# A four-block image kernel: row sums ahead of normalisations, clearing in pieces and hats placed by GpSimd at the end of the third block

## What is computed

```python
def _gn(v, G=32, eps=1e-05):               # per image, groups of two channels
    g = v.reshape(B_, G, C_ // G, H_, W_)
    return ((g - mean(g)) / sqrt(var(g) + eps)).reshape(v.shape)

# third block: attention of all 1024 pixels of an image with each other
e1, e2, asm = (prelu(conv1x1(x, w, b)) for w, b in ...)    # 32, 32 and 64 channels
score = softmax(einsum('nci,ncj->nij', e1, e2), axis=2)
out = einsum('nij,ncj->nci', score, asm)

# fourth block: bilinear shift by theta_s per channel, then 64 -> 64 channels
s = z1*(1-dy)*(1-dx) + z2*(1-dy)*dx + z3*dy*(1-dx) + z4*dy*dx
return einsum('bchw,oc->bohw', s * w_dw, w_pw)

x = x + L0(_gn(x)); x = x + L1(_gn(x)); x = x + L2(_gn(x)); x = x + L3(_gn(x))
```

## Time and profile before

| | before |
|---|---|
| median of 3 runs | 831.44 us (829.63 to 832.01) |
| the profiled execution | 829.34 us, span in the profile 827.5 us |
| PE / DVE / ACT / POOL busy | 84% / 72% / 48% / 50% |

### The profile page before, as it was taken

The page is one execution under the profiler, slowest core; times in us unless marked ns, Lnnn a source line. Parts: engine busy times, 40 slices in busy tenths (PEclk is TensorE's granted clock), DMA queues, the critical chain, the costliest instruction groups (busy, mean ns, idle before and its releaser), DMA issues.

```text
span 827.5 us, 9121 instructions
## 1 busy us (share of the span) xinstructions
PE 693.6 (84%) x2566; PEld 349.4 (42%) x2566; DVE 597.5 (72%) x943; ACT 398.0 (48%) x653; POOL 410.8 (50%) x242
## 2 busy tenths in 40 slices
PE   0875887887459999897989999998999999966787
PEld 0332322222147777574433434343434333225783
DVE  5686899999642325685787868685868787798746
ACT  1768557756211002103547474646566565735571
POOL 3123677677242115101695949494968768542100
PEclk9987899999769999997999999999999999987899
DMA  7000000000000000203303020120303030000005
GB/s 294 0 0 0 1 0 0 0 0 0 0 0 1 0 0 15 63 0 77 76 1 77 1 58 21 31 47 2 76 0 77 0 76 0 1 0 1 1 1 204
DMA packets 7961, 24.90 MB, mean 30 GB/s; under 512 B 2032, under 2 KB 2032, under 8 KB 7792
## 3 DMA queue, kind: packets, MB, share of 16 engines
q1 hardware_dynamic: 7920, 24.45, 10.7%
HBM read 6.09 MB, written 4.19 MB: 12 GB/s over the span
## 4 chain that ended last, share of the span: by engine, by line
PE 49%; DVE 30%; issue 12%; ACT 4%; POOL 2%; DMA 1%; SPq 1%; DVEq 1%; ACTq 0%; POOLq 0%
PE PS L1356 12%; PE PS L1433 10%; PE PS L1400 7%; PE PS L1422 4%; DVE SM L621 3%; PE PS L1381 3%; DVE PS L458 2%; DVE RB L467 2%; PE PS L1391 2%; DVE X L492 1%; PE PS L1268 1%; PE PS L1567 1%; PE PS L1363 1%; PE PS L1595 1%; DVE PS L475 1%
## 5 line engine op out<-in xcount | busy, mean ns | idle before, releaser
L621 DVE TENSOR_REDUCE SM<-PS 128x1 f32<-128x512 f32 x256 | 172.8, 687 | 78.1 <-PE PS L1400 74.1
L988 ACT ACTIVATE RB<-PS 128x512 f32<-128x512 f32 x256 | 139.2, 598 | 108.6 <-PE PS L1422 104.2
L1185 POOL TENSOR_TENSOR RB<-RB 128x1024 f32<-128x1024 f32 x66 | 156.3, 2385 | 20.8 <-ACT RB L988 12.8
L1400 PE MATMUL PS<-R 96*128 96x512 f32 x256 | 123.3, 482 | 13.8 <-DVE SM L621 10.0
L1356 PE MATMUL PS<-R,WS 128*128 128x512 f32 x432 | 119.0, 422 | 4.1 <-ACT R L952 4.1
L1356 PEld LDWEIGHTS PS<-R,WS 128*128 128x128 f32 x432 | 83.1, 193 | 30.9 <-issue 9.3
L1422 PE MATMUL PS<-R 98*128 98x512 f32 x256 | 87.6, 419 | 8.6 <-ACT R L994 4.1
L1400 PEld LDWEIGHTS PS<-R 96*128 96x128 f32 x256 | 48.9, 192 | 95.2 <-issue 49.8
L1433 PE MATMUL PS<-RB 128*64 128x512 f32 x320 | 87.1, 628 | 0.0
L1296 PE MATMUL PS<-RA,W 128*128 (+1 forms) x128 | 67.8, 658 | 21.1 <-DVE RB L467 15.1
L1422 PEld LDWEIGHTS PS<-R 98*128 98x128 f32 x256 | 47.7, 193 | 36.0 <-ACT RB L988 17.8
(11 more groups left out here) (171 smaller groups left out, 1172.4 us busy)
## 6 DMA issues: line engine op xcount, KB each, us to landing
R<-WS SPq DMA_DIRECT2D x84, 128.0 KB, 2.3
X<-x SPq DMA_DIRECT2D x8, 512.0 KB, 10.0
out<-X SPq DMA_DIRECT2D x7, 512.0 KB, 2.6
R<-R SPq DMA_DIRECT2D x24, 128.0 KB, 2.3
W<-pack SPq DMA_DIRECT2D x1, 1273.0 KB, 8.1
RB<-pack SPq DMA_DIRECT2D x1, 576.0 KB, 12.8
out<-X SPq DMA_DIRECT2D x2, 256.0 KB, 2.4
```

What stands on the lines that cost most here:

```text
L621: v.tensor_reduce(MX[:, par, tile, h:h + 1], bank(2 + h), AX.X, ALU.max)\
L988: act(slot[:, h * HALF:(h + 1) * HALF], bank(4 + h), ACT.Exp).then_inc(s["p_ready"], 1)
L1185: i = g.tensor_tensor(out, out, PT[j % SLOTS][par], ALU.add)
L1400: mm(bank(2 + h), stack(b, par, 0)[0:96, tile * P:(tile + 1) * P], stack(b, par, 1)[0:96, h * HALF:(h + 1) * HALF]).then_inc(s["s_mm"], 1)
```

## The change

On DVE, the two hats of group 0 are made right after the first adds of pair 7, ahead of pair 6's residual; the coefficients of `GN3A` come ahead of pair 6's statistics; DVE normalises pairs 0, 1 and 6 only, with an `add` between, and ACT pairs 2 to 5 and 7; DVE's `place(g)` is for the x matrices of groups 0, 2 and 3; both hats of group 1 follow the last `add`. The transposes use banks 2 to 5 instead of 0 to 3, and the group for `GN3B` on PE stands at n=7, not n=5. GpSimd clears the matrices in eight pieces of 128x1024, five of them ahead of its row sums of pair 7, and places the hats `(0,0)`, `(1,0)`, `(1,1)`, and makes and places the y hats of groups 2 and 3 itself; ACT has no part in the hats any more. Core of the diff (semaphores `g3_dve`, `g3_act`, `am_pool` take the place of `g3_done`, `am_act`):

```diff
@@ vector @@
+            hat(0, 0)
+            hat(0, 1)
             for h in range(2):
                 scaled(q, h)
                 residual(q, h)
             add(2)
-            hat(0, 0)
+            coefs_shift(GN3A, 0, q)
             end_stats(q, 0)
             end_stats(q, 1)
-            coefs_shift(GN3A, 0, q)
             add(3)
-            for p in range(q):
-                if p == 3:
-                    add(4)
-                normed3(p)
+            normed3(0)
+            add(4)
+            normed3(1)
             for j in (5, 6, 7):
                 add(j)
-            hat(0, 1)
             hat(1, 0)
+            hat(1, 1)
...
             normed3(q - 1)
-            v.wait_ge(s["am_zero"], 1)
-            place(0, 0)
-            place(0, 1)
+            place(0)
...
-                if n == 0:
-                    hat(1, 1)
-                    v.wait_ge(s["am_zero"], 2)
-                    place(1, 0)
-                    place(1, 1)
                 if n in (2, 6):
                     hat(2 + n // 6, 1)
                 if n in (4, 8):
-                    place(1 + n // 4, 1)
+                    place(1 + n // 4)
@@ scalar @@
             attend(PAIRS - 1, 1, lead=False)
+            a.wait_ge(s["coef_ready"], GN3A + 1)
+            for p in range(2, PAIRS - 2):
+                normed3(p)
             for h in range(2):
                 product_out(PAIRS - 1, h)
...
-                if n == 6:
+                if n == 8:
                     a.wait_ge(s["coef_ready"], GN3B + 1)
...
-                if n in (3, 7):
-                    place(2 + n // 7)
@@ gpsimd @@
+            def clear(k):
+                g.memset(RB[:, k * L:(k + 1) * L], 0.0).then_inc(s["am_zero"], 1)
                 if p == PAIRS - 1:
                     power(GN3A, 0, PAIRS - 2)
+                    g.wait_ge(s["v_done"], 2 * PAIRS)
+                    g.wait_ge(s["pv_done"], 2 * CHUNKS * (PAIRS - 2))
+                    for k in (13, 14, 15):
+                        clear(k)
+                    g.wait_ge(s["sum_mm"], 2 * PAIRS - 2)
+                    for k in (8, 9):
+                        clear(k)
...
+            def hat(gr):
+                tv = mat("thy", C)[:, gr * CG:(gr + 1) * CG].unsqueeze(2).to_broadcast([P, CG, WW])
+                link(g.tensor_tensor(HATP, grid, tv, ALU.add))
+                link(g.tensor_scalar(HAT[2], HATP, 0.0, 1.0, ALU.min, ALU.mult))
+                link(g.tensor_scalar(HATP, HATP, 0.0, 1.0, ALU.max, ALU.mult))
+                link(g.tensor_tensor(HAT[2], HAT[2], HATP, ALU.subtract))
+            def place(gr, a):
+                for q in range(4):
+                    r = slice(32 * q, 32 * q + 32)
+                    i = g.tensor_scalar(AM[gr % 2][a][r, :, 32 * q:32 * q + 32], HAT[2 * min(gr, 1) + a][r],
+                                        1.0 if gr >= 2 else 0.0, 0.0, ALU.add, ALU.max)
+                    if q < 3:
+                        link(i)
+                i.then_inc(s["am_pool"], 1)
+            g.wait_ge(s["pv_done"], 2 * CHUNKS * PAIRS)
+            clear(12)
+            g.wait_ge(s["sum_mm"], 2 * PAIRS)
+            for k in (10, 11):
+                clear(k)
+            g.wait_ge(s["am_zero"], 8)
+            g.wait_ge(s["hat_done"], 4)
+            place(0, 0)
+            power(GN3B, PAIRS - 2, PAIRS)
+            g.wait_ge(s["pow_done"], GN3B + 1)
+            place(1, 0)
+            place(1, 1)
             for gr in (2, 3):
+                hat(gr)
+                g.wait_ge(s["s1_mm"], (gr - 1) * CG // 4)
+                place(gr, 0)
@@ tensor @@
-            t.wait_ge(s["acc_read"], 2 * PAIRS)
+            t.wait_ge(s["s_read"], 32 * PAIRS)
+            t.wait_ge(s["p_ready"], 32 * PAIRS)
...
-                if n == 5:
+                if n == 7:
                     t.wait_ge(s["x2_done"], 2 * PAIRS)
                     group(GN3B, PAIRS - 2, PAIRS)
```

More of the change, by code:

```diff
@@ L281, in transposed_out @@
             q, xb = divmod(n, 8)
[L282 removed]
+            src = bank(2 + n % 4).rearrange("p (x a c) -> p x a c", x=4, a=2)
             dst = D.rearrange("p c (q a x) -> p q x a c", q=2, a=2)[:, q, 4 * xb:4 * xb + 4]
@@ L731, in hat @@
             def hat(g, a):
+                if g == 2:
+                    v.wait_ge(s["am_pool"], 3)
                 w = HAT[2 * min(g, 1) + a]
@@ L736, in hat, with place @@
                 link(v.tensor_scalar(w, HATV, -1.0, 1.0, ALU.mult, ALU.add))
-                link(v.scalar_tensor_tensor(w, HATV, 1.0, w, ALU.add, ALU.min))
-            def place(g, a):
-                if g >= 2:
+                v.scalar_tensor_tensor(w, HATV, 1.0, w, ALU.add, ALU.min).then_inc(s["hat_done"], 1)
+                v.wait_ge(s["hat_done"], 2 * g + a + 1 if g < 2 else 3 + g)
+            def place(g):
+                if g == 0:
+                    v.wait_ge(s["am_zero"], 8)
+                else:
                     v.wait_ge(s["s2_mm"], (g - 1) * CG // 4)
@@ L800, in _ @@
                 transposed_out(v.tensor_copy, n).then_inc(s["tr_dve"], 1)
+            v.wait_ge(s["am_pool"], 1)
             for n in range(16):
@@ L1041, in _, with normed3 @@
             attend(PAIRS - 1, 1, lead=False)
+            def normed3(p):
+                act(G3[:, p, :], X[:, p, :], ACT.Identity, scale=SC[:, p:p + 1], bias=SH[:, p:p + 1])\
+                    .then_inc(s["g3_act"], 1)
+            a.wait_ge(s["coef_ready"], GN3A + 1)
+            for p in range(2, PAIRS - 2):
+                normed3(p)
             for h in range(2):
@@ L1052, in _ @@
             for n in list(range(8)) + list(range(8, 16, 2)):
-                if n == 6:
+                if n == 8:
                     a.wait_ge(s["coef_ready"], GN3B + 1)
-                    act(G3[:, PAIRS - 1, :], X[:, PAIRS - 1, :], ACT.Identity, scale=SC[:, PAIRS - 1:PAIRS],
-                        bias=SH[:, PAIRS - 1:PAIRS]).then_inc(s["g3_done"], 1)
+                    normed3(PAIRS - 1)
                 a.wait_ge(s["tr_mm"], n + 1)
                 transposed_out(copy, n).then_inc(s["tr_act"], 1)
-            def place(g):
-                a.wait_ge(s["dist_done"], g - 1)
-                link(act(HAT[2], HAT[2], ACT.Abs))
-                a.wait_ge(s["s2_mm"], (g - 1) * CG // 4)
-                for q in range(4):
-                    r = slice(32 * q, 32 * q + 32)
-                    i = act(AM[g % 2][0][r, :, 32 * q:32 * q + 32], HAT[2][r], ACT.Relu, bias=ONE[r], scale=-1.0)
-                i.then_inc(s["am_act"], 1)
             for n in range(16):
@@ L1222, in _ @@
                 sums(p)
-            for n in range(2):
-                if n == 0:
-                    g.wait_ge(s["sum_mm"], 2 * PAIRS)
-                else:
-                    g.wait_ge(s["x2_done"], 2 * PAIRS)
-                g.memset(RB[:, PAIRS * L + 2 * n * CG * P:PAIRS * L + 2 * (n + 1) * CG * P], 0.0)\
-                    .then_inc(s["am_zero"], 1)
-                g.wait_ge(s["am_zero"], n + 1)
-                if n == 0:
-                    power(GN3B, PAIRS - 2, PAIRS)
-                    g.wait_ge(s["pow_done"], GN3B + 1)
@@ new lines, in place @@
+            def place(gr, a):
[6 more added lines that the diff above has]
+                i.then_inc(s["am_pool"], 1)
+                g.wait_ge(s["am_pool"], gr + a + 1 if gr < 2 else gr + 2)
@@ L1240, in _ @@
-                need(g, s["am_act"], gr - 2)
-                g.tensor_tensor(HAT[2], grid, tv, ALU.add).then_inc(s["dist_done"], 1)
-                g.wait_ge(s["dist_done"], gr - 1)
+                hat(gr)
+                g.wait_ge(s["s1_mm"], (gr - 1) * CG // 4)
+                place(gr, 0)
         @block.tensor
@@ L1535, in _ @@
                 if xb == 0:
-                    t.wait_ge(s["g3_done"], 4 * q + 4)
+                    t.wait_ge(s["g3_dve"], 2 + q)
+                    t.wait_ge(s["g3_act"], 2 + 3 * q)
                 if n >= 4:
@@ L1552, in shift_y @@
                     g = n // 4
-                    t.wait_ge(s["am_dve"], (2, 4, 5, 6)[g])
-                    need(t, s["am_act"], g - 1)
+                    t.wait_ge(s["am_pool"], (1, 2, 4, 5)[g])
                 need(t, s["s1_copied"], n - 1)
@@ L1561, in shift_x @@
             def shift_x(n):
+                if n % 4 == 0:
+                    g = n // 4
+                    t.wait_ge(s["am_pool" if g == 1 else "am_dve"], (1, 3, 2, 3)[g])
                 t.wait_ge(s["s1_copied"], n + 1)
@@ L1569, in shift_x @@
                 i.then_inc(s["s2_mm"], 1)
+            t.wait_ge(s["acc_read"], 2 * PAIRS)
             t.wait_ge(s["tr_act"], 12)
```

14 lines of the change are left out of this document (6 added, 8 removed).

## The result

| | before | after |
|---|---|---|
| median | 831.42 us (827.37 to 832.59, 8 runs) | 838.44 us (834.50 to 840.74, 8 runs) |
| the profiled execution | 829.34 us, span 827.5 us | 840.74 us, span 838.9 us |

The ratio is 1.0086, with a 95% interval of 1.0061 to 1.0111: the change costs 7.0 us. The prediction was 823.2 us and faster; both the size and the sign are wrong.

A forecast was written before the change was run, and what follows sets the result against it. PE, busy 84% of the span, bounds the kernel, so time returns only where it idles. Gains followed through six points reach 8.2 us at the last x product; off the median 831.44 that gives 823.2 us, range 817.5 to 830.5.

The forecast's parts named there:

- 1, row sums on PE: PE's row sums of pair 7 start at 736.3 instead of 738.58: gain 2.3 us.
- 2, DVE's residual of pair 7: DVE's residual of pair 7, before at 742.34, follows two hats after the adds, at 740.0: gain stays 2.3 us.
- 3, transposes of group 8: PE's transposes of group 8 start at 749.35 instead of 753.79, with POOL's placings at 0.79 each: gain 4.4 us.
- 4, first shift product: The shift's first product on PE, before at 760.97, comes at 758.3; the stretch loses 1.7, gain 2.7 us.
- 5, second x product: The shift's second x product on PE comes at 761.9 instead of 769.77, DVE having no placing at n=0: gain 7.9 us.
- 6, end of the last x product: PE's last x product of the shift ends at 792.0 instead of 800.24: gain 8.2 us.
- The tail behind: From the end of the last x product to the kernel's end: 27.3 us, the same as before.
- Clears 8 and 9: Rival: these clears push POOL's row sums back, so no gain there; 825.5 us, chance 0.05.
- The price of POOL's placing instruction: GpSimd's placing of hats: 0.65 us, 0.79 each with the wait behind its predecessor; bounds 0.45 and 1.27.
- one meeting on the port at n=4: In the shift, DVE's four placings wait for POOL's placings and hat, taking 5.3 us; PE loses 4.0.
- GpSimd becomes the bound: Rival: placings at 1.27 plus 0.14 us delay power by 2.1 and make DVE wait; 835.5 us, chance 0.14.
- threshold of 1.08: Price in us per GpSimd placing instruction from about which the rival of GpSimd as the bound decides.

The follow-up runs named there:

- e7: The kernel before with only GpSimd's clearing in eight pieces, all other orders unchanged: 827.23 us, ratio 0.9954 to the kernel before.
- e1: The kernel before with 22 extra GpSimd instructions on an unused tile behind the last x product, to price each operation: 833.84 us, one run.
- e8: The kernel before with 13 extra GpSimd instructions beside 16 pairs on DVE, behind the last x product: 864.28 us.
- e9: e5 with ACT only making the y hats of groups 2 and 3 and GpSimd placing them by copies: 819.75 us, ratio 0.9869 to the kernel before.
- e2: The changed kernel with GpSimd's power for GN3B ahead of its first placing instead of behind it: 842.03 us, ratio 1.0127 to the kernel before.
- e10: The changed kernel with GpSimd's 12 placings of groups 0 and 1 as copies, the maximum done by DVE: 828.01 us, ratio 0.9953 to the kernel before.
- e5: e3 with GpSimd's 12 placings as copies and the maximum made once per hat by DVE: 818.88 us, ratio 0.9842 to the kernel before.
- e4: The changed kernel with all placing as before the change (DVE and ACT), the rest of the change kept: 823.47 us, ratio 0.9898 to the kernel before.
- e3: The changed kernel with the y hats of groups 2 and 3 finished and placed by ACT again: 825.70 us, ratio 0.9934 to the kernel before.
- e6: e4 with group 1 placed by GpSimd's copies, its hats clamped by DVE: 824.21 us, ratio 0.9919 to the kernel before.

## Why the prediction was wrong, by its own points

Counted from the common start; "gain" is time that the changed kernel is earlier.

| point | gain predicted | gain measured |
|---|---|---|
| 1, row sums on PE | 2.3 | 3.5 |
| 2, DVE's residual of pair 7 | 2.3 | 3.5 |
| 3, transposes of group 8 | 4.4 | 2.7 |
| 4, first shift product | 2.7 | 2.1 |
| 5, second x product | 7.9 | 7.0 |
| 6, end of the last x product | 8.2 | -6.4 |

(Point 1, for one: 738.58 - 702.68 = 35.90 before, 740.02 - 707.62 = 32.40 after. Point 6: 800.24 - 702.68 = 97.56 and 811.56 - 707.62 = 103.94.) The tail behind is 27.3 in both, as said.

*Points 1 and 2 held*, with 1.2 us more than forecast: POOL's row sums and DVE's instructions between them took 17.5 us (718.19 to 735.71), not 14.3 + 5.2 = 19.5. Clears 8 and 9 ahead of POOL's sums didn't cancel this gain, but alone they come with 1.1 us of loss (e7).

*Point 3 is the step that failed.* "The price of POOL's placing instruction is not in the trace": it took the nearest row of the same kind, 0.65 us, with 1.27 as the upper bound, and noted that no row had the maximum. It measured 1.93 (e1: 1.95 for this operation, 0.77 for the row's kind, multiply and add with operands per partition). The row chosen shared the instruction's name, not its operation, and the bound wasn't one: nothing in the trace limited an operation that no row had. The wait for the power, given as a condition of the rival, is there: 4.12 us. That point 3 still gained 2.7 is a sum of three: the 3.5 of point 2, less 3.4 because `power` comes 9.93 us behind the residual and not 6.56, plus 2.6 behind it, where the normalisation is down from 3.88 to 1.01 us (forecast: about 1.5).

*Points 4 and 5* look nearly right, but by luck: errors cancel. The shift's transposes start 1.7 us later than forecast, though the row sums gave 1.2 more; against that, DVE's four placings took 2.33 and not 4.9, since the slow instruction doesn't hold DVE all the time (e8).

*Point 6 is where the time goes.* The stretch from point 5 takes 43.9 us in place of 30.5. Forecast was one meeting on the port at n=4, worth 4.0 (its own terms, three of 0.79 and one of 1.35, give 3.7). That mechanism is real, and over-sized. Where POOL copies, it costs 1.25 and 0.50 (e9: DVE 3.11 in place of 1.71). In the changed kernel it costs PE no wait at n=4 and 1.34 at n=8, where DVE's placings meet POOL's hat. The other waits are for POOL's *queue*: 2.76 (1.93 of it for the semaphore, the rest DVE's hat slowed beside POOL's), 3.40 and 4.10, and the low clock behind them. Priced right, it could be read off before: 12 placings, two hats of some 7 and 8 more placings are about 55 us of work from 745.71, and PE, free of waits, would want the last matrix 39 us after that (y of n=2 at 766.81, and 10 steps of 1.79 more).

*The rival "GpSimd becomes the bound"* is what happened by its name and by its first step, the late power; its way from there is not. It let DVE wait on each of POOL's instructions, so that the shift would start 3.1 us later than before, and it started 2.1 earlier. The time went later, by the queue's total (e2, e10). So its 835.5 at a price of 1.27 lies near 838.44 by luck: at 1.93 the same way would have given more. Its threshold of 1.08 was tested by no run; there are only prices of 0.66 and 1.93. It had a chance of 0.14 because the bound was taken for one. The Trainium skill (GPSIMD Engine Reference, section 3.1) gives 769 ns for 512 elements in a tight loop. e1 agrees for multiply and add with operands per partition (770) and not for a maximum (1498 alone). The reason that the Trainium skill gives there for leaving elementwise work to DVE, that GpSimd is slower, holds for each instruction here, for copies too (0.66 against 0.43). But e5 shows that the slower engine can still be the right place, when it is idle and DVE is on the path.

The account of the change, from the medians: clearing in pieces with DVE's order and the normalisations on ACT -8.1 (e4; how it splits is open, see e7), hats and placing on GpSimd with the maximum +15.2 (after against e4), together +7.0. Here each kernel is taken against the kernel before of its own set. Placing on GpSimd with copies and ACT for groups 2 and 3 is -4.6 (e5 against e4). Four kernels show where the +15.2 lies: taking the maximum from the 12 placings of groups 0 and 1 is worth 10.1 with GpSimd's own hats behind them (e10 against after) and only 6.8 without (e5 against e3); giving groups 2 and 3 back to ACT is worth 12.9 behind slow placings (e3 against after) and 9.7 behind copies (e5 against e10). Neither alone is the cause; what counts is the sum in one queue. Counted in the profiles from the common start to the end of the span, after, e2 to e6, e9 and e10 differ from before by what their medians differ, within 1.3 us. **e5, 818.88 us, beats both kernels**: by 12.7 us, 1.58% (1.41 to 1.75), the one before.

## What to carry to other kernels

Price an instruction by its operation, not by its name and shape; where no row has the operation, its upper bound is open, and what counts is the price from which it decides (1.08 us by the prediction's reckoning, not tested). Ask then for the *total* of the queue between its first input and the last taker, ahead of who meets whom on a port: moving the power ahead (e2) cured the wait that one saw and made the kernel no faster. And where work is to move to a slower engine, send it the part that this engine does at its best price (the copy) and leave the other (the maximum, once per hat) where it costs 0.43 us.
